# Turning 36 groups of y in a graph network's first pass and copying them back in its table pass

## The chip, the cores and the metric

One core of one Trainium2 chip. The time is device microseconds from start to end of one launch; the median of several runs is compared.

## The reference, cut to what matters

Two residual graph layers over N = 50000 nodes (128 features) and E = 25000 edges sorted by destination.

```python
h = relu(layernorm(x))
msg = concat([h[dst], h[src] - h[dst]]) @ W0 + b0
x = x + relu(segment_max(msg, dst, N))            # empty segments give 0
h = relu(layernorm(x))
a = softmax over edges of (concat([h[src] @ Wn, h[dst] @ Wn, edge @ We]) @ Watt)
g = gelu(gelu(concat([h[src], h[dst], edge]) @ Wm1 + b) @ Wm2 + b) @ Wm3 + b
x = x + scatter_add(a * g, dst)
```

The last lines leave out the projections' biases, which the kernel does add. Below, y is x after the first layer at an edge's destination, and then its normalized form.

## The kernel before, in words

The edges are cut in 49 groups of 4 tiles of 128 (G = 49, LAST = 48, GE = 512; the last group is padded). `big` holds one segment of 512 columns per group for the whole kernel (L311). Five engines each run a list of stages written out by hand, tied by semaphores. `over(engine, signal, n)` (L61) waits until the signal's stage of group n is over. `in_order` (L71) runs step m of a list: each stage at its own lag, in the order of the list. Four-slot rings (SLOTS) hold gathered rows.

**First pass.** GpSimd's `gather_a` (L518) gathers x's source and destination rows, 8 indirect DMAs a group, and waits for slot n-4 to be normalized, copied and kept. VectorE (L814) takes statistics of group n when its data are there, makes scale and shift for a pair of groups in a chain of small instructions (`norm_links`, L663; every second group), applies them (`applies`, L710: xn), scans the messages for the running maximum (`max_a`, L746) and adds x (`add_y`, L758). TensorE (L1028) runs per step: `turn_a` of the group before (8 transpositions of xn), half of the key products, `messages_a` (L1008, waits for the scan of the group before), the other half, `back_a`. ScalarE (L1184) runs: `copy_a`, `relu_a`, the signs of half the keys, `bias_a`, the other half, `norm_y_a` at lag LATE = 9, which normalizes y's rows in `big` in place, group n in step n + 9. The last 9 groups of y are normalized at the start of the table pass (`norm_y_b`, L1193).

The keys find for each edge a row of the table to which the first pass spilled y and x; SyncE's queue carries these spills and the copy of x to the output.

**Table pass.** It runs from the last group to the first (`mirrored`, L91): step n works on group 48 - n. GpSimd's `gather_b` (L537) gathers 4 tiles of the table a group and waits for xn of n-4. VectorE (L892) runs per group: xn of n-2, `spread_b(n-2)` (L869), statistics of n; after each odd n the chain for a pair. `spread_b` scans y from the bank to `hd` backwards, which spreads each destination's y to all its edges; it waits for `b_turned_y` of n, for `b_first` of n-2, whose products read that half of `hd`, and for the scan before. TensorE (L1073) runs per step n:

```python
                turn_b(n)
                turn_y_b(n + 1)
                if n >= 2:
                    turn_g_b(n - 2)
                if n >= 1:
                    first_b(n - 1)
                if n >= 2:
                    second_b(n - 2)
```

`turn_y_b` (L1031) transposes y's 4 tiles from `big` to bank 2 or 3. All transpositions have L968 in the profile, the helper `turn`. `first_b` (L1044) is 12 products of 129 columns (L1053 to L1055), `second_b` one of 512 (L1067). ScalarE (L1226) runs per step n: `relu_b(n)` (L1187), `norm_y_b(n + 2)`, `keep_g_b(n - 2)` (L1212), both halves of `gelu1_b(n - 1)`, `gelu2_b(n - 2)`, which overwrites the group's segment of `big`.

After the last group come a maximum, the exponentials, and the **output pass** (L962, L1134, L556): weighting, a scan, back turns, 196 indirect scatters by GpSimd, which wait also for the copy of x.

Of the kernel before, what the change touches and what calls it, by code (L numbers as in the profile page):

```python
# [10 lines left out]
ACT = mybir.ActivationFunctionType  # L11
AX_X = mybir.AxisListType.X

P = 128
TPG = 4
GE = TPG * P
# [44 lines left out]
def over(eng, signal, n, each=1):  # L61

    if n < 0:
        return
    if isinstance(signal, list):
        eng.wait_ge(signal[n % SLOTS], each * (n // SLOTS + 1))
    else:
        eng.wait_ge(signal, each * (n + 1))
# [11 lines left out]
def gnn_kernel(nc, x, edge_attr, W, idx_in, src_pad, dst_pad, eaT_in, wpack, out):  # L80
# [3 lines left out]
    G = TILES // TPG  # L84
# [6 lines left out]
    def mirrored(n):  # L91
        return LAST - n

    with ExitStack() as ctx:
# [3 lines left out]
        def sem(name):  # L98
            return ctx.enter_context(nc.semaphore(name))
# [51 lines left out]
        big = sb("big", [P, EP])  # L151
# [32 lines left out]
        bank = [ctx.enter_context(nc.psum_tensor(f"bank{i}", [P, 512], F32)) for i in range(8)]  # L184
# [66 lines left out]
        a_relu = sem("a_relu")  # L251
# [6 lines left out]
        a_links_y = sem("a_links_y")  # L258
        b_links_y = sem("b_links_y")
        normed_y = sem("normed_y")  # L260
        s_idx_y = sem("s_idx_y")
        s_ones_row = sem("s_ones_row")

# [1 line left out]
        b_gathered = ring("b_gathered")  # L265
        b_normed = sem("b_normed")
        b_turned_y = sem("b_turned_y")
        b_turned = sem("b_turned")
        b_hd = sem("b_hd")
        b_hs = sem("b_hs")  # L270
# [37 lines left out]
        def tile(buf, u, j):  # L308
            return buf[:, u, j * P:(j + 1) * P]

        def segment(n):  # L311
            return big[:, n * GE:(n + 1) * GE]
# [11 lines left out]
        PIECES = N // PIECE  # L324
        assert (N - PIECES * PIECE) % 16 == 0
        LATE = 9
        A_GATHERS = 2 * TPG * 16
        GATHERS = TPG * 16
        QUARTER = EP // 4
# [5 lines left out]
        def _(sp):  # L335
# [12 lines left out]
            def phases(src, eaT):  # L348
# [30 lines left out]
                def keep_xs(n):  # L379
                    over(sp, a_gathered, n, A_GATHERS)  # L380
                    sp.dma_start(table_rows(EP, n), by_tile(xs[:, n % SLOTS, :])).then_inc(a_kept[n % SLOTS], 16)
# [177 lines left out]
        def _(dve):  # L559
# [254 lines left out]
            for n in range(0, LAST):  # L814
# [5 lines left out]
                reach_a(n + 1)  # L820
                over(dve, a_gathered, n, A_GATHERS)
                stats(n, 0, tiles_a(n))
# [16 lines left out]
            add_y(LAST - 5)  # L839
            over(dve, a_gathered, LAST, A_GATHERS)  # L840
            stats(LAST, 0, tiles_a(LAST))
# [26 lines left out]

            def spread_b(n):  # L869
                d, m = n % 2, mirrored(n)  # L870
                over(dve, b_turned_y, n)
                over(dve, b_first, n - 2, 2)
                over(dve, b_hd, n - 1)
                dve.tensor_tensor_scan(hd[:, d, ::-1], flags[:, m * GE + 1:(m + 1) * GE + 1][:, ::-1],  # L874
                                       bank[2 + d][:, ::-1], hd[:, 1 - d, 0:1], ALU.mult, ALU.max
                                       ).then_inc(b_hd, 1)
# [88 lines left out]
        def _(pe):  # L965
            def turn(dest, source):
                for j in range(TPG):
                    ins = pe.transpose(dest[:, j * P:(j + 1) * P], source(j), ident[:, :])  # L968
                return ins
# [31 lines left out]
            def turn_a(n):  # L1001
                d = n % 2
                over(pe, a_normed, n)
                over(pe, a_relu, n - 2)
                turn(bank[d], lambda j: tile(xn, d, j))
                turn(bank[2 + d], lambda j: tile(xn, d, TPG + j)).then_inc(a_turned, 1)

            def messages_a(n):  # L1008
                d = n % 2
# [9 lines left out]
            def back_a(n):  # L1019
# [4 lines left out]
                else:  # L1024
# [1 line left out]
                turn(maxima(n), lambda j: tile(run, d, j)).then_inc(a_back, 1)  # L1026

            in_order(G, [(1, turn_a), (0, lambda n: keys_a(n, 0)), (2, messages_a), (0, lambda n: keys_a(n, 1)),  # L1028
                         (3, back_a)])

            def turn_y_b(n):  # L1031
                d, m = n % 2, mirrored(n)
                if n < LATE:
                    pe.wait_ge(normed_y, G - LATE + n + 1)
                over(pe, b_hd, n - 2)
                turn(bank[2 + d], lambda j: big[:, m * GE + j * P:m * GE + (j + 1) * P]).then_inc(b_turned_y, 1)

# [99 lines left out]
        def _(act):  # L1137
            act.dma_start(wp[:, :], wpack).then_inc(s_weights, 16)

            def copy_a(n):  # L1140
                over(act, a_gathered, n, A_GATHERS)
                act.activation(segment(n), xd[:, n % SLOTS, :], ACT.Copy).then_inc(a_copied, 1)

            def signs_a(n, h):
                over(act, a_keys, 2 * n + h)
                over(act, a_signs, 2 * n + h - 2)
                dest = bank[7] if h else bank[5]
                keys = dest[:, 0:2 * (KW + 1)].rearrange("p (q k) -> p q k", k=KW + 1)
                t = n * TPG + 2 * h
                for q in range(2):  # L1150
                    act.activation(compared[:, 2 * h + q, :], keys[:, q, 0:KW], ACT.Sign, bias=src_key[:, t + q:t + q + 1],  # L1151
                                   scale=-1.0, accum_out=signs[:, t + q:t + q + 1])
                act.activation(key_base[:, t:t + 2], keys[:, :, KW], ACT.Copy).then_inc(a_signs, 1)
# [13 lines left out]
            def norm_y(m):  # L1167
                for j in range(TPG):
                    c = m * TPG + j
                    rows_y = big[:, c * P:(c + 1) * P]  # L1170
                    ins = act.activation(rows_y, rows_y, ACT.Identity, scale=y_scale[:, c:c + 1],  # L1171
                                         bias=y_shift[:, c:c + 1])
                ins.then_inc(normed_y, 1)

            def norm_y_a(n):
                if n < G - LATE:
                    act.wait_ge(a_links_y, n // 2 + 1)
                    over(act, a_spilled, n, 16)
                    norm_y(n)

            act.wait_ge(s_weights, 16)
            act.wait_ge(s_keys, 1)
            act.wait_ge(s_unsorted, 1)
            in_order(G, [(0, copy_a), (1, relu_a), (0, lambda n: signs_a(n, 0)), (2, bias_a),  # L1184
                         (0, lambda n: signs_a(n, 1)), (LATE, norm_y_a)])

            def relu_b(n):  # L1187
                d = n % 2
                over(act, b_turned, n)
                over(act, b_first, n - 2, 2)  # L1190
                act.activation(hs[:, d, :], bank[d][:, :], ACT.Relu).then_inc(b_hs, 1)

            def norm_y_b(n):  # L1193
                if n < LATE:
                    m = mirrored(n)
                    if m > LAST - 7:
                        act.wait_ge(b_links_y, (n + 1) // 2 + 1)
                    else:
                        act.wait_ge(a_links_y, m // 2 + 1)
                    over(act, a_spilled, m, 16)  # L1200
                    norm_y(m)

            def gelu1_b(n, h):
                d, t = n % 2, mirrored(n) * TPG + 2 * h
# [20 lines left out]
            norm_y_b(1)  # L1225
            for n in range(0, LAST):  # L1226
                relu_b(n)
                norm_y_b(n + 2)
                if n >= 2:
                    keep_g_b(n - 2)  # L1230
                if n >= 1:
                    gelu1_b(n - 1, 0)
                    gelu1_b(n - 1, 1)
                if n >= 2:
                    gelu2_b(n - 2)
# [97 lines left out]
```

## Time and profile before

| | |
|---|---|
| median of 3 runs | 1078.14 us (1077.06 to 1079.75) |
| the profiled execution, its own time | 1078.1 us |
| its span, first to last instruction | 1076.5 us |
| mean granted TensorE clock | 0.784 |
| busy: TensorE, weight loads, VectorE, ScalarE, GpSimd | 63%, 42%, 70%, 39%, 71% |

Busy times overlap, since the engines run side by side. "DMA_INDIRECT" on POOL is the time in which GpSimd issues a gather or scatter, not the transfer. In a timeline, a row may gather several instructions (x4); the bracket is the idle time of the engine before it and what ended it. "issue" says that the profile shows nothing that was waited for.

### The profile page before, as it was taken

To read this page: it belongs to the slowest core of one execution; us is meant where nothing else is said; L and a number is where in the kernel's file an instruction comes from. 1 tells how busy PE (TensorE), PEld (TensorE's weight loads), DVE (VectorE), ACT (ScalarE), POOL (GpSimd) and SP (SyncE) were. 2 spreads that over 40 slices of the span, in tenths; PEclk is the share of its full clock that TensorE was granted. 3 is DMA by queue.
4 is the path that set the end of the run, shared out by engine and by line. 5 is a ranking of instruction groups with operands and counts; after the bars stand their busy time and mean duration, and the time that the engine had idled before them with its cause. 6 is when DMAs were issued, how large, how long until landed. Compare 5 with 4: busy or idle time off the path is not lost.

```text
span 1076.5 us, 13373 instructions
## 1 busy us (share of the span) xinstructions
PE 677.4 (63%) x3369; PEld 451.5 (42%) x3369; DVE 754.1 (70%) x2588; ACT 421.2 (39%) x1239; POOL 759.8 (71%) x796
## 2 busy tenths in 40 slices
PE   1356576565565555467549999999996555555520
PEld 1233343333333333334248888888873222222210
DVE  3468688688688788788988888888847555555540
ACT  1234445645645646646437555555552000000000
POOL 5777777777777777776277777777705777777775
PEclk9977767878887878867759999999999656555555
DMA  4645545445445555454324444443424344444420
GB/s 145 226 116 151 149 141 161 150 141 157 151 145 157 151 145 149 152 149 139 107 66 127 140 136 117 139 137 115 143 84 135 121 139 140 137 137 144 156 75 32
DMA packets 65044, 145.52 MB, mean 135 GB/s; under 512 B 17994, under 2 KB 19009, under 8 KB 64054
## 3 DMA queue, kind: packets, MB, share of 16 engines
q1 hardware_dynamic: 39734, 96.46, 27.3%
q0 software_dynamic: 25088, 47.56, 17.2%
q10 hardware_dynamic: 144, 0.63, 0.2%
q8 instruction: 28, 0.46, 0.2%
q14 instruction: 50, 0.41, 0.1%
HBM read 109.79 MB, written 64.26 MB: 162 GB/s over the span
## 4 chain that ended last, share of the span: by engine, by line
POOL 33%; DVE 30%; issue 19%; PE 8%; DMA 8%; ACT 1%; POOLq 0%; DVEq 0%; ACTq 0%
POOL out_dram L552 14%; POOL xs L484 11%; POOL xd L484 8%; DVE xn L714 8%; DVE bst L660 5%; DMA xd<-in_x_dram,idx_dst 5%; PE bank L968 4%; DVE hd L874 3%; DVE run L755 3%; DMA out_dram<-aux,idx_out 2%; DVE newton L671 2%; DVE rstd L671 2%; PE bank L1053 1%; DVE big L761 1%; PE bank L1054 1%
## 5 line engine op out<-in xcount | busy, mean ns | idle before, releaser
L552 POOL DMA_INDIRECT out_dram<-aux,idx_out x196 | 193.0, 985 | 95.2 <-issue 56.7
L484 POOL DMA_INDIRECT xs<-table,idx_y x196 | 186.4, 951 | 76.6 <-issue 55.7
L484 POOL DMA_INDIRECT xs<-in_x_dram,idx_src x196 | 187.2, 955 | 66.1 <-issue 60.6
L484 POOL DMA_INDIRECT xd<-in_x_dram,idx_dst x196 | 189.7, 968 | 59.8 <-issue 59.5
L1016 PE MATMUL bank<-hs,wp 128*128 128x512 f32 x98 | 86.0, 974 | 172.5 <-DVE run L755 172.4
L660 DVE BATCH_NORM_STATS2 bst<-xs 128x6 f32<-128x128 f32 x392 | 84.3, 278 | 105.7 <-DMA xd<-in_x_dram,idx_dst 105.1
L1100 PE MATMUL bank<-big,wp 128*128 128x512 f32 x98 | 86.3, 979 | 95.4 <-DVE bank L940 94.9
L968 PE MATMUL bank<-ident,xn 128*128 128x128 f32 x588 | 90.0, 293 | 60.8 <-DVE xn L714 59.8
L968 PEld LDWEIGHTS bank<-ident,xn 128*128 128x128 f32 x588 | 72.2, 152 | 99.1 <-DVE xn L714 86.2
L714 DVE TENSOR_SCALAR xn<-xs,mean,rstd 128x128 f32<-128x128 f32 x392 | 111.4, 366 | 1.8
L1164 ACT ACTIVATE bank<-bank,wp 128x512 f32<-128x512 f32 x49 | 32.5, 663 | 204.6 <-PE bank L1017 204.6
L956 DVE SCALAR_TENSOR_TENSOR aux<-bank,sm,xd 128x512 f32<-128x512 f32 x49 | 36.7, 748 | 106.2 <-DMA out_dram<-aux,idx_out 106.2
L1016 PEld LDWEIGHTS bank<-hs,wp 128*128 128x128 f32 x98 | 21.1, 268 | 184.8 <-issue 155.2
L968 PEld LDWEIGHTS bank<-ident,run 128*128 128x128 f32 x392 | 68.5, 192 | 66.9 <-DVE run L948 49.7
L968 PE MATMUL bank<-ident,run 128*128 128x128 f32 x392 | 87.1, 364 | 13.1 <-DVE run L948 11.7
L1151 ACT ACTIVATE compared<-bank,src_key 128x252 bf16<-128x252 f32 x196 | 90.9, 476 | 4.7 <-PE bank L997 4.6
L1171 ACT ACTIVATE big<-big,y_shift,y_scale 128x128 f32<-128x128 f32 x196 | 80.5, 492 | 9.6 <-DVE y_shift L735 9.6
L1017 PE MATMUL bank<-hd,wp 128*128 128x512 f32 x98 | 82.1, 936 | 0.0
L874 DVE TENSOR_TENSOR_SCAN hd<-flags,hd,bank 128x512 f32<-128x512 uint8 x49 | 62.5, 1276 | 27.3 <-issue 27.3
L997 PE MATMUL bank<-key_parts,m_a 100*128 100x253 bf16 x392 | 74.4, 324 | 7.8 <-DVE m_a L743 7.8
L1053 PE MATMUL bank<-wp,aux 65*128 65x129 f32 x392 | 76.6, 276 | 0.0
L1054 PE MATMUL bank<-wp,hd 128*128 128x129 f32 x392 | 76.3, 275 | 0.0
(138 smaller groups left out, 1363.3 us busy)
## 6 DMA issues: line engine op xcount, KB each, us to landing
out_dram<-in_x_dram SPq DMA_DIRECT2D x48, 512.0 KB
table<-xs SPq DMA_DIRECT2D x49, 256.0 KB, 2.2
table<-big SPq DMA_DIRECT2D x49, 256.0 KB, 4.1
xd<-table SPq DMA_DIRECT2D x49, 256.0 KB, 2.8
xn<-exps_dram SPq DMA_DIRECT2D x45, 256.0 KB, 3.3
aux<-in_src_dram SPq DMA_DIRECT2D x49, 200.0 KB
aux<-in_eaT_dram SPq DMA_DIRECT2D x49, 128.0 KB, 3.1
xs<-in_x_dram,idx_src POOLq DMA_INDIRECT x196, 3.5
```

The costliest lines, as they stand in the source:

```text
L484: pool.indirect_dma_start(tile(buf, u, j), None, source, bass.IndirectOffsetOnAxis(ap=index[:, c:c + 1], axis=0)).then_inc(done[u], 16)
L552: pool.indirect_dma_start(out, bass.IndirectOffsetOnAxis(ap=idx_out[:, c:c + 1], axis=0), tile(aux, u, j), None, bounds_check=last_row, oo ...
L660: ins = dve.bn_stats(bst[:, n % 2, first + j, :], t)
L714: ins = dve.tensor_scalar(tile(xn, k, j), t, mean[:, pair, k, j:j + 1], rstd[:, pair, k, j:j + 1], ALU.subtract, ALU.mult)
L874: dve.tensor_tensor_scan(hd[:, d, ::-1], flags[:, m * GE + 1:(m + 1) * GE + 1][:, ::-1], bank[2 + d][:, ::-1], hd[:, 1 - d, 0:1], ALU.mult ...
L968: ins = pe.transpose(dest[:, j * P:(j + 1) * P], source(j), ident[:, :])
L1016: pe.matmul(dest, weight("w0_src"), hs[:, d, :], start=True, stop=False)
L1017: pe.matmul(dest, weight("w0_dst"), hd[:, d, :], start=False, stop=True).then_inc(a_msg, 1)
L1053: pe.matmul(dest, aux[0:DE + 1, u, j * P:(j + 1) * P], weight("w1_edge"), start=True, stop=False)
L1054: pe.matmul(dest, tile(hd, d, j), weight("w1_dst"), start=False, stop=False)
L1100: pe.matmul(bank[2 + n % 2][:, :], weight("w3"), segment(n), start=True, stop=True).then_inc(c_third, 1)
L1151: act.activation(compared[:, 2 * h + q, :], keys[:, q, 0:KW], ACT.Sign, bias=src_key[:, t + q:t + q + 1], scale=-1.0, accum_out=signs[:, t ...
```

## The change

- First pass: TensorE gets a stage `turn_y_a` at lag 10, last in its step. For groups 0 to 35 (TURNED = 49 - 9 - 4 = 36) it transposes the normalized y from `big` to bank 0 or 1, after the relu that emptied that bank. ScalarE gets `keep_y_a` at lag 10, last in its step, which copies the bank back over the segment in `big`. `turn_a(n)` waits for the copy that empties its bank.
- Table pass: for groups below 36 `turn_y_b` does nothing; ScalarE's `copy_y_b(n + 1)`, after `relu_b(n)`, copies the segment to bank 2 or 3, and `spread_b` waits for that copy. The first 13 groups of this pass (48 down to 36) stay as they were.

```diff
--- before.py
+++ after.py
@@ -258,6 +258,8 @@
         a_links_y = sem("a_links_y")
         b_links_y = sem("b_links_y")
         normed_y = sem("normed_y")
+        a_turned_y = sem("a_turned_y")
+        a_kept_y = sem("a_kept_y")
         s_idx_y = sem("s_idx_y")
         s_ones_row = sem("s_ones_row")
 
@@ -265,6 +267,7 @@
         b_gathered = ring("b_gathered")
         b_normed = sem("b_normed")
         b_turned_y = sem("b_turned_y")
+        b_copied_y = sem("b_copied_y")
         b_turned = sem("b_turned")
         b_hd = sem("b_hd")
         b_hs = sem("b_hs")
@@ -324,6 +327,7 @@
         PIECES = N // PIECE
         assert (N - PIECES * PIECE) % 16 == 0
         LATE = 9
+        TURNED = G - LATE - 4
         A_GATHERS = 2 * TPG * 16
         GATHERS = TPG * 16
         QUARTER = EP // 4
@@ -868,7 +872,7 @@
 
             def spread_b(n):
                 d, m = n % 2, mirrored(n)
-                over(dve, b_turned_y, n)
+                over(dve, b_turned_y if m >= TURNED else b_copied_y, n if m >= TURNED else TURNED - 1 - m)
                 over(dve, b_first, n - 2, 2)
                 over(dve, b_hd, n - 1)
                 dve.tensor_tensor_scan(hd[:, d, ::-1], flags[:, m * GE + 1:(m + 1) * GE + 1][:, ::-1],
@@ -1002,8 +1006,16 @@
                 d = n % 2
                 over(pe, a_normed, n)
                 over(pe, a_relu, n - 2)
+                over(pe, a_kept_y, min(n - LATE - 1, TURNED - 1))
                 turn(bank[d], lambda j: tile(xn, d, j))
                 turn(bank[2 + d], lambda j: tile(xn, d, TPG + j)).then_inc(a_turned, 1)
+
+            def turn_y_a(n):
+                m = n + LATE + 1
+                if n < TURNED:
+                    pe.wait_ge(normed_y, n + 1)
+                    over(pe, a_relu, m - 2)
+                    turn(bank[m % 2], lambda j: big[:, n * GE + j * P:n * GE + (j + 1) * P]).then_inc(a_turned_y, 1)
 
             def messages_a(n):
                 d = n % 2
@@ -1026,12 +1038,14 @@
                 turn(maxima(n), lambda j: tile(run, d, j)).then_inc(a_back, 1)
 
             in_order(G, [(1, turn_a), (0, lambda n: keys_a(n, 0)), (2, messages_a), (0, lambda n: keys_a(n, 1)),
-                         (3, back_a)])
+                         (3, back_a), (LATE + 1, turn_y_a)])
 
             def turn_y_b(n):
                 d, m = n % 2, mirrored(n)
                 if n < LATE:
                     pe.wait_ge(normed_y, G - LATE + n + 1)
+                if m < TURNED:
+                    return
                 over(pe, b_hd, n - 2)
                 turn(bank[2 + d], lambda j: big[:, m * GE + j * P:m * GE + (j + 1) * P]).then_inc(b_turned_y, 1)
 
@@ -1178,11 +1192,16 @@
                     over(act, a_spilled, n, 16)
                     norm_y(n)
 
+            def keep_y_a(n):
+                if n < TURNED:
+                    over(act, a_turned_y, n)
+                    act.activation(segment(n), bank[(n + LATE + 1) % 2][:, :], ACT.Copy).then_inc(a_kept_y, 1)
+
             act.wait_ge(s_weights, 16)
             act.wait_ge(s_keys, 1)
             act.wait_ge(s_unsorted, 1)
             in_order(G, [(0, copy_a), (1, relu_a), (0, lambda n: signs_a(n, 0)), (2, bias_a),
-                         (0, lambda n: signs_a(n, 1)), (LATE, norm_y_a)])
+                         (0, lambda n: signs_a(n, 1)), (LATE, norm_y_a), (LATE + 1, keep_y_a)])
 
             def relu_b(n):
                 d = n % 2
@@ -1200,6 +1219,11 @@
                     over(act, a_spilled, m, 16)
                     norm_y(m)
 
+            def copy_y_b(n):
+                if mirrored(n) < TURNED:
+                    over(act, b_hd, n - 2)
+                    act.activation(bank[2 + n % 2][:, :], segment(mirrored(n)), ACT.Copy).then_inc(b_copied_y, 1)
+
             def gelu1_b(n, h):
                 d, t = n % 2, mirrored(n) * TPG + 2 * h
                 half = bank[4 + h][:, 0:2 * (P + 1)].rearrange("p (q c) -> p q c", c=P + 1)
@@ -1225,6 +1249,7 @@
             norm_y_b(1)
             for n in range(0, LAST):
                 relu_b(n)
+                copy_y_b(n + 1)
                 norm_y_b(n + 2)
                 if n >= 2:
                     keep_g_b(n - 2)
```

## Rows read from the trace of the kernel before

**Rows 1.** Busy time by window: length, each engine (instructions), granted clock, DMA share, GB/s.

```profile
9.30:512.07 502.77, 286.73 (x1130) 169.84 (x1130) 378.55 (x1483) 257.18 (x819) 376.92 (x392) 0.79 0.51 152
...
532.22:780.42 248.20, 223.40 (x1688) 193.38 (x1689) 209.16 (x832) 133.70 (x345) 186.41 (x196) 0.94 0.42 124
780.42:816.16 35.74, 32.35 (x215) 24.94 (x214) 18.88 (x65) 20.37 (x48) 0.00 (x0) 1.00 0.22 73
816.16:1076.50 260.34, 120.89 (x281) 54.93 (x279) 126.12 (x141) 0.00 (x0) 193.03 (x196) 0.58 0.40 124
...
642.70:652.80 10.10, 9.93 (x77) 8.58 (x77) 8.40 (x33) 5.46 (x15) 7.65 (x8) 1.00 0.45 132
```

**Rows 2.** Timeline of GpSimd in the table pass: start us, duration us, what.

```profile
597.43 0.95 POOL L484 DMA_INDIRECT xs<-table,idx_y  x1 [0.30 <-issue]
...
676.63 0.95 POOL L484 DMA_INDIRECT xs<-table,idx_y  x1 [1.42 <-issue]
...
736.90 0.95 POOL L484 DMA_INDIRECT xs<-table,idx_y  x1 [0.31 <-DVE xn L714]
...
764.45 0.95 POOL L484 DMA_INDIRECT xs<-table,idx_y  x1 [0.30 <-issue]
...
779.46 0.94 POOL L484 DMA_INDIRECT xs<-table,idx_y  x1 [0.30 <-issue]
```

**Rows 3.** Timeline of a pair of groups in the table pass, all engines.

```profile
641.49 1.11 DVE L714 TENSOR_SCALAR xn<-xs,mean,rstd 128x128 f32<-128x128 f32 x4
...
642.66 0.65 PE L968 MATMUL bank<-ident,xn 128*128 128x128 f32 x4 [0.16 <-DVE xn L714]
...
642.75 0.94 POOL L484 DMA_INDIRECT xs<-table,idx_y  x1 [0.30 <-DVE xn L714]
...
643.36 0.60 ACT L1191 ACTIVATE hs<-bank 128x512 f32<-128x512 f32 x1
...
646.97 1.28 DVE L874 TENSOR_TENSOR_SCAN hd<-flags,hd,bank 128x512 f32<-128x512 uint8 x1 [1.25 <-issue]
...
651.58 1.11 DVE L714 TENSOR_SCALAR xn<-xs,mean,rstd 128x128 f32<-128x128 f32 x4
```

**Rows 4.** One piece of the chain of waits, then timeline at the table pass's end.

```profile
540.99 2.49 DMA xs<-table,idx_y
...
769.28 0.84 DVE L660 BATCH_NORM_STATS2 bst<-xs 128x6 f32<-128x128 f32 x4
...
779.37 0.66 PE L968 MATMUL bank<-ident,xn 128*128 128x128 f32 x4 [0.52 <-DVE xn L714]
...
784.27 0.60 PE L968 MATMUL bank<-ident,xn 128*128 128x128 f32 x4
...
784.71 0.60 PE L968 MATMUL bank<-ident,big 128*128 128x128 f32 x4
...
797.96 0.60 PE L968 MATMUL bank<-ident,xn 128*128 128x128 f32 x4
```

**Rows 5.** Timeline of the first pass, all engines.

```profile
303.16 0.94 POOL L484 DMA_INDIRECT xs<-in_x_dram,idx_src  x1 [0.30 <-DVE xn L714]
...
307.30 1.28 PE L1016 MATMUL bank<-hs,wp 128*128 128x512 f32 x2 [2.80 <-DVE run L755]
...
310.32 0.66 ACT L1164 ACTIVATE bank<-bank,wp 128x512 f32<-128x512 f32 x1 [3.38 <-PE bank L1017]
...
312.13 1.64 ACT L1171 ACTIVATE big<-big,y_shift,y_scale 128x128 f32<-128x128 f32 x4
...
314.63 0.87 DVE L660 BATCH_NORM_STATS2 bst<-xs 128x6 f32<-128x128 f32 x4 [3.69 <-DMA xd<-in_x_dram,idx_dst]
...
323.34 1.09 POOL L484 DMA_INDIRECT xs<-in_x_dram,idx_src  x1 [0.30 <-DVE xn L714]
...
500.31 2.05 PE L1016 MATMUL bank<-hs,wp 128*128 128x512 f32 x2 [3.46 <-DVE run L755]
...
502.15 1.91 PE L1017 MATMUL bank<-hd,wp 128*128 128x512 f32 x2
```

## The prediction, made blind

> **What bounds the kernel now.** I read the busy time by stage first [rows 1]. The kernel is three passes one behind the other: first pass (9 to 512 us), table pass (gathers from 532 to 780, its drain to 816), output pass (816 to the end). In the output pass GpSimd issues 196 scatters in 260 us and nothing of it is touched, so time won or lost before 816 moves the end one for one.
>
> In the table pass two loops run at almost the same speed, and that is the point of the case. The first is GpSimd's: a gather starts every 1.25 us, its idle time is the fixed 0.30 between two of them, four make a group [rows 2]. From 736.90 to 779.46 it starts 34 gathers, 1.252 us each, so a pair of groups costs 10.01 at the free pace. The second is a loop through VectorE and TensorE, once per pair [rows 3]: xn of an even group is ready at 642.60; TensorE transposes xn (642.66), y and the kept gelu, and runs first_b of the group before; the scan of the next group, which writes the buffer that first_b reads, starts at 646.97, when first_b is over (the page says "issue"; by the code, L872, it is b_first); then come statistics, the rsqrt chain, and xn again at 651.58. 651.58 - 641.49 = 10.09. So TensorE has 4.3 us in a loop of 10.09, VectorE 5.8, and GpSimd, at 10.01 to 10.1, runs alongside with its ring of four full: the gather at 642.75 needs exactly the xn that ended at 642.60.
>
> In the first pass GpSimd is the wall: 16 gathers from 303.16 to 323.34, 20.18 us, 10.09 per group; VectorE waits 3.69 us per pair for data, TensorE 2.80 for a scan, ScalarE 3.38 for the message product [rows 5]. The releaser "DVE xn" beside the 0.30 is misleading there: by the code gather n waits for xn of n-4, which ended a group earlier.
>
> **The change part by part.** All against the profiled execution: span 1076.5, own time 1078.1, which is also the median of the runs shown (1078.14).
>
> 1. Table pass, removed: the 4 transpositions of y in 36 of 49 groups (n from 13, as 48 - n < 36). Four at full clock take 784.71 - 784.27 = 0.44 us [rows 4]. All lie in TensorE's 4.3 us stretch, or in the other half of the pair where they cost nothing, so the loop becomes 10.09 - 0.44 = 9.65.
>
> 2. Table pass, added: one ScalarE copy of 512 columns per group. Cost 0.60, from relu of the same size [rows 3]; bounds 0.6 and 0.7, nothing in between decides. It stands after relu (643.36 to 643.96), so it ends at 644.6 and keep_g at 645.2. The scan that needs it starts at 646.97 now, 646.53 after; the second product that needs keep_g comes after first_b. Its wait for the scan of n-2 is long over. ScalarE is 54% busy in this pass (133.7 of 248.2 us) [rows 1], so 0. If that cover were gone, at most 0.6 per pair would return.
>
> 3. So the wall of the table pass becomes GpSimd. What does the pass gain? Two terms.
> a) **GpSimd's pace.** From its gather at 597.43 (group 13) to the last at 779.46 are 143 intervals in 182.0 us [rows 2]. At the free pace, 143 x 1.252 = 179.0, so 3.0 us is the most that is to be had. Worst: the first pass's pace, 20.18 / 16 = 1.261, plus the single 1.1 us pause before 676.63, of which I find no cause: 180.3 + 1.1 = 181.4; and if gathers collide with VectorE more often than now, nothing at all or 0.5 lost. I take 0.7, with the pause kept, because the nearest stretch is that with both engines in step.
> b) **The drain.** At full ring, data wait for VectorE. The last gather of group 45 is issued at 764.45 and data land 2.49 later [rows 2, 4]: 766.94. Its statistics start at 769.28, so 2.3 us are in hand. A loop of 9.65 against a feed of 10.01 to 10.1 gains 0.4 per pair; from group 13 to 45 are 16 pairs, 6 us, more than enough to use that up. Then turn_b(45) starts at 777.0 instead of 779.37. From there TensorE is unbroken to 797.96 [rows 4] with three y transpositions in the way (46, 47, 48), 3 x 0.44 = 1.3. xn of 46, 47 and 48 move up by the same 2.3 and stay ahead. Drain: 2.3 + 1.3 = 3.6.
> Sum: 3.6 + 0.7 = 4.3 us faster.
>
> 4. First pass, added on TensorE: 36 x 4 transpositions, 0.44 at full clock, 0.88 at half, in step n+10 behind back_a. Added on ScalarE: 36 copies of 0.6. Added waits: the copy waits for that turn, and behind it on ScalarE stand copy_a and relu_a; turn_a(n) waits for the copy, and behind it on TensorE stand keys and messages. The path from one scan to the next message product, at the clock seen: 0.15 + messages 3.02 (307.30 to 310.32) + bias and signs 1.81 (to 312.13) + norm_y 1.64 + copy 0.6 + turn_a 1.1 (eight transpositions, 0.88 at full clock over 0.79) + keys 0.6 (taken as four) = 8.9, below 10.09 per group [rows 5]. What it delays (relu_a, copy_a by 0.6 to 2.8 us) has three groups of ring before GpSimd sees it. So 0; the 2.80 and 3.38 of idle shrink.
>
> 5. TensorE's clock. It is granted in full (2.4 GHz) all through the drain, where TensorE is 32.35 of 35.74 us busy, 91%, and at a mean of 0.79 in the first pass [rows 1]. Now a pair of the table pass has 9.93 us of it in 10.10 [rows 1]; after the change (9.93 - 0.88) / 10.05, about 90%, which is what the drain has. I count no loss. A loss begins when TensorE's 3.86 in the loop grows past 4.2, a mean clock under 0.92.
>
> 6. No DMA, no SyncE or GpSimd instruction moves. SyncE's eaT loads wait for first_b and come no later.
>
> **The rivals.**
> A. *GpSimd slows in its new phase.* The gather at 303.16 took 0.94, the one at 323.34 took 1.09, next to an xn [rows 5]. If data-bound step puts one such on each of 18 pairs beyond now, 18 x 0.15 = 2.7, and the pace term goes from +0.7 to -2.0: total 3.6 - 2.0 = 1.6 faster, 1076.5. The Trainium skill, SBUF — State Buffer, "Who interferes with whom", says that a tensor_scalar of VectorE in a two-port mode and GpSimd lock each other out of a shared port pair for the whole instruction. By that rule xn holds up gathers wherever they meet; the lengthened gather in the trace agrees in kind, though it lost 0.15 us and not a whole xn. Chance 0.2.
> B. *Data is not ready sooner*, since another wait of 0.4 us stands in VectorE's loop, so the catching up fails. Then only 1.3 of the drain is left, 1076.8. For it: both loops agree so closely that I may have the order of cause wrong. Against it: statistics at 769.28 show no wait. The Trainium skill, Perfetto Trace Analysis, "Identifying the Most-Contended Engine", judges TensorE by its weight loads. Taken so, it has 22% to spare in this pass (193.4 of 248.2) [rows 1] and removing its work should give nothing; I hold that a loop needs no full engine. Chance 0.15.
> C. *Slower: first pass.* The path of step 4 at half clock throughout: 0.15 + 3.7 (four passes of 0.92, from 500.31 to 502.15 are two) + 1.81 + 1.64 + 0.6 + 1.76 + 0.9 (keys, taken as four transpositions) = 10.56, over 10.09 by 0.47, 36 times: 17 us, total 17 - 4.3 = 12.8 slower, 1091. It decides once TensorE's three parts in it exceed 5.9 us, a mean clock near 0.54; 0.79 is seen, and more work is there, not less. Chance 0.09.
> D. *The change doesn't do what it says*, the scan still waiting for TensorE through the copy: the copy's input is 100 us old, so this can only be ScalarE late, at 0.6 per pair: no gain in the loop, as B. Inside B's chance.
>
> **How the numbers follow.** The likeliest case (0.56): 1078.1 - 4.3 = 1073.8, own range 1071.6 (pace term 3.0, 6.5 won) to 1074.8. A run of this kernel can tell 0.3%, 3.2 us, from no change: below 1074.9 is faster. A and B (0.35) end inside that, C slower. For 8 in 10 I reach up to A and B with some room, 1077.5, and down to 1071.2; C is left out. Faster 0.56, same 0.35, slower 0.09.
>
> **What would show it.** Right: table pass at 10.0 to 10.1 per pair still, but with VectorE's statistics waiting for gathers from about group 30 on, and the scan's "issue" wait of 1.25 down to 0.8; TensorE busy near 90% in it; last gather within 778 to 780.5; first scatter 4 us sooner, at 812; first pass unchanged to 0.5 us. Wrong: no DMA wait before statistics (B); a last gather after 780.5 (A); first pass past 512.6, or waits of VectorE for the bias (C); a granted clock under 1.00 between 600 and 780 (5).

## The result and the profile after

| | median | lowest to highest | runs |
|---|---|---|---|
| before | 1077.16 us | 1076.69 to 1079.75 | 7 |
| after | 1072.44 us | 1071.18 to 1076.93 | 7 |

The ratio is 0.9955, interval 0.9943 to 0.9966: 4.7 us faster (3.7 to 6.1). The forecast was 1073.8, faster by 4.3.

The profiled execution of after is the slowest of its seven, 1076.93 us (span 1075.3), only 1.2 under the profiled one of before. The seven runs of after go with the mean granted TensorE clock: 1071.18 at 0.800, 1072.44 at 0.787, 1076.93 at 0.773. The 29 runs of before beside e9 to e12 don't: 1076.59 at 0.784, 1080.50 at 0.799. The profiled execution of after lies far above the median, so its trace has to be read with care; a second trace of the same kernel, e7_after_again (1073.91 us, clock 0.786), stands beside it.

Busy time by window of after, where the forecast's steps can be looked up (first pass, a stretch behind it, a stretch of the table pass, table pass to the last gather, drain, output pass; the columns are those of [rows 1]):

```profile
9.30:512.07 502.77, 302.37 (x1260) 188.79 (x1261) 377.43 (x1481) 276.72 (x851) 376.82 (x392) 0.78 0.52 152
508.50:513.00 4.50, 4.26 (x12) 2.01 (x13) 2.78 (x14) 2.00 (x7) 0.00 (x0) 0.62 0.97 303
534.15:782.16 248.01, 212.44 (x1567) 182.41 (x1568) 210.96 (x837) 148.36 (x380) 184.90 (x196) 0.93 0.42 124
782.16:815.32 33.16, 29.77 (x192) 22.36 (x191) 17.54 (x60) 20.35 (x48) 0.94 (x1) 1.00 0.24 81
815.32:1075.30 259.98, 122.53 (x281) 55.71 (x279) 126.14 (x141) 0.00 (x0) 192.65 (x196) 0.57 0.41 125
655.00:660.00 5.00, 5.00 (x33) 5.00 (x31) 2.69 (x9) 2.05 (x5) 3.72 (x5) 0.66 0.23 66
```

TensorE and ScalarE have taken on the turning and keeping in the first pass (302.4 and 276.7 us against 286.7 and 257.2 [rows 1]), and the pass is as long as before. The drain has fallen from 36.70 to 33.16, measured from the last gather. Two windows, 508.5 to 513 and 655 to 660, show the clock well under 1.00; before has 1.00 in the first of them.

Next, a table of the traces on which the argument rests, in microseconds: the gap from the last gather of the first pass to the first one of the table pass, the table pass from its first gather to its last, the drain from there to the first scatter, and the rest.

| kernel | gap | table pass | drain | rest | span |
|---|---|---|---|---|---|
| before | 27.71 | 247.24 | 36.70 | 260.34 | 1076.5 |
| after | 29.84 | 248.01 | 33.16 | 259.98 | 1075.3 |
| e7, after once more | 29.59 | 245.51 | 33.56 | 259.85 | 1072.3 |
| e12, table part alone | 27.71 | 246.94 | 33.17 | 259.84 | 1072.1 |
| e9, first-pass part alone | 27.88 | 246.89 | 36.74 | 259.83 | 1075.4 |
| e10, three groups turned | 27.71 | 246.78 | 35.43 | 259.79 | 1074.7 |
| e11, twenty groups turned | 28.17 | 247.92 | 34.81 | 259.79 | 1075.0 |

**Where the gain is.** In the drain, in every trace with the whole table part: 3.1 to 3.5 us. No trace shows where the rest of the 4.7 comes from; the fastest runs of after (1071.18 to 1072.61) were not traced. **What hides it in the profiled execution.** First the gap. Timeline of after, TensorE, behind the first pass:

```profile
508.74 1.96 PE L1028 MATMUL bank<-hs,wp 128*128 128x512 f32 x2 [1.79 <-DVE run L759]
510.49 1.90 PE L1029 MATMUL bank<-hd,wp 128*128 128x512 f32 x2
```

Before has the same four matmuls at full clock:

```profile
508.95 1.10 PE L1016 MATMUL bank<-hs,wp 128*128 128x512 f32 x2 [1.61 <-DVE run L755]
509.88 1.02 PE L1017 MATMUL bank<-hd,wp 128*128 128x512 f32 x2
```

The window's clock of 0.62 is a mean: TensorE is granted either 2.4 or 1.2 GHz (1.00 or 0.50), and these rows run at 0.50 for most of it. Here nothing is hidden any more: gathers have ended, and scan, messages and bias wait for each other in turn. The next scan starts at 513.12 after 1.77 of waiting for the bias, and the first table gather comes 2.1 us later against the last one of the first pass. Second, the table pass of after. One piece of its chain of waits, the flight of the last gather of step 21:

```profile
644.04 6.06 DMA xs<-table,idx_y
```

Then timelines; VectorE and TensorE, then GpSimd:

```profile
650.13 0.87 DVE L664 BATCH_NORM_STATS2 bst<-xs 128x6 f32<-128x128 f32 x4 [1.79 <-DMA xs<-table,idx_y]
...
654.68 0.66 PE L972 MATMUL bank<-ident,xn 128*128 128x128 f32 x4 [2.44 <-DVE xn L718]
...
655.62 0.64 PE L1067 MATMUL bank<-wp,aux 65*128 65x129 f32 x2
656.05 0.64 PE L1068 MATMUL bank<-wp,hd 128*128 128x129 f32 x2
...
660.19 1.28 DVE L878 TENSOR_TENSOR_SCAN hd<-flags,hd,bank 128x512 f32<-128x512 uint8 x1 [2.46 <-issue]
...
666.67 0.94 POOL L488 DMA_INDIRECT xs<-table,idx_y  x1 [1.59 <-DVE xn L718]
...
679.31 0.94 POOL L488 DMA_INDIRECT xs<-table,idx_y  x1 [1.70 <-issue]
```

The statistics wait 1.79 for a gather. This isn't yet the wait of the forecast, for step 21 is only the ninth changed step: the gather took 6.06 us from issue to landing, where [rows 4] have 2.49. Then TensorE is idle for 2.44, its clock is at half for 3.4 us, and the products come 0.43 apart instead of the 0.22 of full clock; the scan behind them waits 2.46, so VectorE is late again and GpSimd finds its ring full (1.59 instead of 0.30). That cost 1.3 us. That the idle time brought the clock down is argued from the order alone. TensorE in e12, where the same gather took 4.88:

```profile
652.38 0.66 PE L972 MATMUL bank<-ident,xn 128*128 128x128 f32 x4 [2.26 <-DVE xn L718]
```

After an idle time of 2.26 the clock stays at 1.00 there. The 1.70 at 679.31 is a pause like the 1.42 that before has at the same place, the 114th gather of the pass [rows 2]; e7 has none. 1.3 + 1.4 is 2.7, and after's table pass is 2.5 longer than e7's.

### The profile page after: what moved, and what is told of

It reads as the page before. It is cut to its first block, busy times and chain, and to the rows that moved or that the text cites. A ratio compares the mean times of both kernels' runs of the same rounds, so it can differ in the third digit from the quotient of the medians.

```text
span 1075.3 us, 13481 instructions
## 1 busy us (share of the span) xinstructions
PE 681.5 (63%) x3369; PEld 458.6 (43%) x3369; DVE 754.1 (70%) x2588; ACT 456.5 (42%) x1311; POOL 758.9 (71%) x796
## 4 chain that ended last, share of the span: by engine, by line
POOL 37%; DVE 27%; issue 20%; DMA 8%; PE 6%; ACT 1%; POOLq 0%; DVEq 0%; ACTq 0%
POOL out_dram L556 15%; POOL xs L488 14%; POOL xd L488 8%; DVE xn L718 7%; DVE bst L664 5%; DMA xd<-in_x_dram,idx_dst 4%; DVE run L759 3%; PE bank L972 2%; DMA out_dram<-aux,idx_out 2%; DVE hd L878 2%; DVE newton L675 2%; DMA xs<-table,idx_y 2%; DVE big L765 1%; DVE rstd L675 1%; PE bank L1067 1%
## 5 line engine op out<-in xcount | busy, mean ns | idle before, releaser
L972 PE MATMUL bank<-ident,xn 128*128 128x128 f32 x588 | 98.4, 313 | 152.8 <-ACT big L1198 85.5
L972 PEld LDWEIGHTS bank<-ident,xn 128*128 128x128 f32 x588 | 76.9, 160 | 194.4 <-issue 105.7
L1028 PE MATMUL bank<-hs,wp 128*128 128x512 f32 x98 | 83.3, 946 | 75.9 <-DVE run L759 75.2
L972 PEld LDWEIGHTS bank<-ident,run 128*128 128x128 f32 x392 | 65.0, 184 | 68.2 <-DVE run L952 49.6
L972 PE MATMUL bank<-ident,run 128*128 128x128 f32 x392 | 83.6, 353 | 14.9 <-DVE run L952 11.9
L1001 PE MATMUL bank<-key_parts,m_a 100*128 100x253 bf16 x392 | 77.1, 333 | 7.7 <-DVE m_a L747 7.7
L878 DVE TENSOR_TENSOR_SCAN hd<-flags,hd,bank 128x512 f32<-128x512 uint8 x49 | 62.5, 1276 | 22.0 <-issue 22.0
L1069 PE MATMUL bank<-wp,hs 128*128 128x129 f32 x392 | 77.0, 279 | 0.0
L1029 PE MATMUL bank<-hd,wp 128*128 128x512 f32 x98 | 73.9, 848 | 0.0
```

What stands on the lines that cost most here:

```text
L1028: pe.matmul(dest, weight("w0_src"), hs[:, d, :], start=True, stop=False)
```

## The experiments

Two theories stood against each other. **L**: the table pass runs at the pace of the loop through VectorE and TensorE, GpSimd beside it at nearly the same pace; shortening the loop leaves GpSimd as the wall, and the gain is what had queued up, plus the drain. **G**: GpSimd alone sets the pace and the loop only follows. Then came **D** and **P**: is the gain in the drain and there at once (D), or does it grow with the number of changed groups (P)?

### The first four: a chip in another condition

e1_first_only copies the kept y to a spare buffer and turns in the table pass as before:

```diff
+        spare = sb("spare", [P, GE])
...
-                over(dve, b_turned_y if m >= TURNED else b_copied_y, n if m >= TURNED else TURNED - 1 - m)
+                over(dve, b_turned_y, n)
...
-                if m < TURNED:
-                    return
...
-                    act.activation(segment(n), bank[(n + LATE + 1) % 2][:, :], ACT.Copy).then_inc(a_kept_y, 1)
+                    act.activation(spare[:, :], bank[(n + LATE + 1) % 2][:, :], ACT.Copy).then_inc(a_kept_y, 1)
...
-                copy_y_b(n + 1)
```

> Only the first pass's half: TensorE turns y of 36 groups, ScalarE copies the bank to a spare buffer of its own, turn_a waits for that copy; the table pass is that of before. Theory D (the whole gain is in the drain behind the last gather; the first pass hides its half): same as before within 1 us, first pass's last gather still near 504.5. Rival C (the first pass pays for the gain): 2 us or more slower than before. Theory K (the transition between the passes is slower or faster by 1 to 2 us by the granted clock alone): the first gather of the table pass anywhere from 532 to 534.5, with the granted clock between 508 and 520 telling which.

e2_table_only leaves the turning and keeping out of the first pass, so the table pass scans y unturned:

```diff
-                over(pe, a_kept_y, min(n - LATE - 1, TURNED - 1))
...
-                         (3, back_a), (LATE + 1, turn_y_a)])
+                         (3, back_a)])
...
-                         (0, lambda n: signs_a(n, 1)), (LATE, norm_y_a), (LATE + 1, keep_y_a)])
+                         (0, lambda n: signs_a(n, 1)), (LATE, norm_y_a)])
```

> Only the table pass's half: no turn in the first pass, ScalarE copies the segments of 36 groups as they are (the turning of these y's is left out) to the bank that VectorE scans. Theory D: 4 to 5.5 us faster than before, as the whole change or up to 1 us better. Rival C: clearly better than the whole change, by 2 us or more.

e3_turned_3 and e4_turned_20 change how many groups are treated the new way, the last 3 and the last 20 steps of the table pass:

```diff
-        TURNED = G - LATE - 4
+        TURNED = 3
```

> The change for 3 groups only, the last three of the table pass (TURNED = 3). Theory D splits the gain of the drain into 1.3 us (three transpositions of y in TensorE's unbroken last stretch) and 2.3 us (a VectorE that has caught up with the gathers before the end): here only the first is left, so 1.3 us faster than before, drain from last gather to first scatter 34.4 instead of 35.7. Rival P (the gain is GpSimd's pace in the steady stretch): no more than 0.3 us. Rival E (the end alone makes it): 3.5 us or more.

> The change for 20 groups (TURNED = 20), the last 20 of the table pass, ten pairs. Theory D: a loop shorter by 0.35 to 0.44 us per pair makes up 3.5 to 4.4 us in ten pairs, which covers the 2.3 to 4 us by which data wait, so the full drain gain of 3.3 to 3.6 us: 3.5 to 4.5 us faster than before, no worse than the whole change. Rival P (pace of the gathers, in proportion to the groups): 20/36 of 4.7, 2.6 us faster.

Measured: beside these four the kernel before itself took 1319.74 us (1301 to 1343, 17 runs), 22% over all its other measurements. The four took 1377.66 (ratio 1.0495, interval 1.0413 to 1.0577), 1323.26 (1.0103, 1.0037 to 1.0169), 1323.05 (1.0081, 1.003 to 1.0131) and 1351.91 (1.0336, 1.0268 to 1.0403). Timeline of e3, TensorE and GpSimd in the first pass:

```profile
305.50 1.75 PE L972 MATMUL bank<-ident,xn 128*128 128x128 f32 x7 [11.04 <-remote]
...
306.28 0.94 POOL L488 DMA_INDIRECT xs<-in_x_dram,idx_src  x1 [3.67 <-remote]
```

The engines stand idle for reasons that the profile puts down to none of this core's work ("remote"), up to 14 us at a time on TensorE; before, after, e7, e9 and e12 have no such wait on any engine. It isn't a matter of one chip: the record gives number 13 for these four and for e5 to e8 too, beside which before took 1078.78. What caused it isn't known, nor why the first-pass part cost most there (58 us). These four runs say nothing about D or P. They were repeated as e9 to e12.

### e5 and e6: GpSimd with a quarter of its work taken away

Three gathers of four per group, in the kernel before (e5) and in the changed one (e6), one run each; the fourth tile keeps old rows:

```diff
-                gather(n, mirrored(n), xs, idx_y, table, b_gathered)
+                u = n % SLOTS
+                for j in range(TPG - 1):
+                    c = mirrored(n) * TPG + j
+                    pool.indirect_dma_start(tile(xs, u, j), None, table,
+                                            bass.IndirectOffsetOnAxis(ap=idx_y[:, c:c + 1], axis=0)
+                                            ).then_inc(b_gathered[u], 16)
...
-                    over(dve, b_gathered, n, GATHERS)
+                    over(dve, b_gathered, n, (TPG - 1) * 16)
```

> The kernel before with 3 gathers per group in the table pass instead of 4 (the fourth tile's gather is left out, so its rows are stale). GpSimd then needs 7.5 us per pair and can't be what sets the pace. Theory L (before, the loop through TensorE and VectorE sets 10.0 to 10.1 us by itself): the period stays 9.9 to 10.1 us. Rival G (GpSimd set it): 9.6 or less.

> The changed kernel with 3 gathers per group in the table pass. Theory L: the loop of TensorE and VectorE is shorter by the four transpositions, 9.60 to 9.75 us per pair in the 36 changed groups, while the first 13 groups still run at 10.0 to 10.1; the table pass ends 6 to 8 us before that of the same edit to the kernel before. Rival G: 9.0 or less, as TensorE's busy time (8.9) would allow.

Measured: e5 1079.16 us, beside 1078.78 for the kernel before; e6 1069.33. Timeline of e5 in the table pass: the first xn of three pairs, and one gather:

```profile
602.13 1.12 DVE L719 TENSOR_SCALAR xn<-xs,mean,rstd 128x128 f32<-128x128 f32 x4
...
612.21 1.11 DVE L719 TENSOR_SCALAR xn<-xs,mean,rstd 128x128 f32<-128x128 f32 x4
...
614.11 0.95 POOL L543 DMA_INDIRECT xs<-table,idx_y  x1 [2.87 <-DVE xn L719]
...
622.28 1.11 DVE L719 TENSOR_SCALAR xn<-xs,mean,rstd 128x128 f32<-128x128 f32 x4
```

GpSimd needs 6 x 1.25 = 7.5 us for a pair now and waits for its ring, 2.87 in the row shown and up to 3.4; the pair still takes 10.07. Theory G falls: a quarter less work for the engine that is 75% busy gave nothing. The same view of e6:

```profile
601.23 1.11 DVE L723 TENSOR_SCALAR xn<-xs,mean,rstd 128x128 f32<-128x128 f32 x4
...
611.30 1.11 DVE L723 TENSOR_SCALAR xn<-xs,mean,rstd 128x128 f32<-128x128 f32 x4
...
620.89 1.11 DVE L723 TENSOR_SCALAR xn<-xs,mean,rstd 128x128 f32<-128x128 f32 x4
...
630.48 1.11 DVE L723 TENSOR_SCALAR xn<-xs,mean,rstd 128x128 f32<-128x128 f32 x4
```

The first pair is still of the old kind, with TensorE's y transpositions: 10.07. From the step where they end it is 9.59. Four transpositions shortened the loop by 0.48 (forecast 0.44). The table pass fell from 244.11 to 236.04: with the feed out of the way the change is worth 9.8 us, twice as much.

### e7: the changed kernel once more

> The changed kernel once more, for a second trace. Theory K (TensorE's granted clock is what differs between the 1076.9 us of the profiled run and the 1071 to 1072.6 of the others): a run near 1071.5 shows the clock in full between 508 and 513, no stretch below full between 640 and 780, the first gather of the table pass near 532.2 and the last at or before 780. Rival: the same clock and the same two late stretches in a run near 1071.5, the difference being somewhere else.

Measured: 1073.91 us, one run. Timeline of e7, VectorE, in the table pass, then GpSimd's last gather and first scatter:

```profile
697.12 0.87 DVE L664 BATCH_NORM_STATS2 bst<-xs 128x6 f32<-128x128 f32 x4 [1.04 <-DMA xs<-table,idx_y]
...
717.23 0.87 DVE L664 BATCH_NORM_STATS2 bst<-xs 128x6 f32<-128x128 f32 x4 [0.82 <-DMA xs<-table,idx_y]
...
739.91 1.11 DVE L718 TENSOR_SCALAR xn<-xs,mean,rstd 128x128 f32<-128x128 f32 x4
...
744.95 1.28 DVE L878 TENSOR_TENSOR_SCAN hd<-flags,hd,bank 128x512 f32<-128x512 uint8 x1 [0.82 <-issue]
...
749.97 1.12 DVE L718 TENSOR_SCALAR xn<-xs,mean,rstd 128x128 f32<-128x128 f32 x4
...
778.89 0.94 POOL L488 DMA_INDIRECT xs<-table,idx_y  x1 [0.30 <-issue]
812.45 1.02 POOL L556 DMA_INDIRECT out_dram<-aux,idx_out  x1 [32.62 <-DVE aux L960]
```

The statistics of steps 31 and 35 wait for data, 1.04 and 0.82, and no others do: the last gathers of these two took 3.58 and 3.63 us to land. From 739.91 to 749.97 a pair takes 10.06; the seven pairs from 700.51 on take 9.57 to 10.67, 9.95 in the mean. The scan's wait is 0.82 where it was 1.25 [rows 3]. VectorE has no arrears left: the last gather of step 41 lands at 746.23 and its statistics start at 746.26. This is the state that the forecast describes. The gap is 29.59, with the clock at 0.63 from 508.5 to 513, as in the profiled execution; the table pass has no fall of the clock and no pause near 677. Theory K's condition, a run near 1071.5, wasn't met. The two late stretches of the table pass account for most of the 3.0 us between the two traces; e7 with before's gap would be near 1072.0, an estimate from the table.

### e8: without the copy to the bank

VectorE scans y from its segment in SBUF, ScalarE's copy of the table pass is left out:

```diff
-                    over(dve, b_turned_y if m >= TURNED else b_copied_y, n if m >= TURNED else TURNED - 1 - m)
+                    if m >= TURNED:
+                        over(dve, b_turned_y, n)
+                    else:
+                        over(dve, a_kept_y, m)
...
-                                       bank[2 + d][:, ::-1], hd[:, 1 - d, 0:1], ALU.mult, ALU.max
+                                       (bank[2 + d] if m >= TURNED else segment(m))[:, ::-1], hd[:, 1 - d, 0:1], ALU.mult, ALU.max
...
-                copy_y_b(n + 1)
```

> The changed kernel without ScalarE's copy in the table pass: VectorE scans the segment in SBUF itself. Theory L: the copy was hidden, so nothing to win by leaving it out, within 0.7 us of the whole change. Rival S (a VectorE scan with both inputs in SBUF is slower, or holds up GpSimd's gathers): the scan over 1.3 us or gathers over 1.27 us apart, and 2 us or more slower than the whole change. Rival A (the copy does cost, relu and keep_g late): 1 us or more faster than the whole change.

Measured: 1091.31 us (1088.39 to 1092.19), ratio 1.0107 (1.0094 to 1.0121), some 17 to 19 us over the whole change. The table pass takes 264.38. Groups by line of e8 between 600 and 780 (two groups), and a piece of its timeline:

```profile
L488 POOL DMA_INDIRECT xs<-table,idx_y x130 | 140.7, 1082 | 39.6 <-issue 32.6 <-DVE xn L718 7.0
...
L881 DVE TENSOR_TENSOR_SCAN hd<-flags,hd,big 128x512 f32<-128x512 uint8 x30 | 38.4, 1281 | 8.8 <-issue 8.7
```

```profile
697.52 1.28 DVE L881 TENSOR_TENSOR_SCAN hd<-flags,hd,big 128x512 f32<-128x512 uint8 x1
...
697.75 1.81 POOL L488 DMA_INDIRECT xs<-table,idx_y  x1 [0.30 <-DVE xn L718]
699.86 0.94 POOL L488 DMA_INDIRECT xs<-table,idx_y  x1 [0.30 <-issue]
```

The same group of gathers in e7, between 600 and 780:

```profile
L488 POOL DMA_INDIRECT xs<-table,idx_y x144 | 136.7, 949 | 43.9 <-issue 40.2 <-DVE xn L718 3.7
```

The scan is as long as ever (1281 ns, from the bank 1276), but a gather that meets it takes 1.81 instead of 0.94, and the mean of all rises from 949 to 1082 ns. 130 gathers fit where e7 has 144. The trace holds its own comparison: in the first 13 groups, where the scan still reads a bank, no gather takes over 1.03; of the 144 behind them 25 take over 1.2, each of them while a scan of a segment runs. Their mean is 0.13 above e7's, and 144 x 0.13 is the 19 us by which this table pass is longer (264.38 against 245.51); TensorE's clock falls in this pass too (0.50 from 677 to 678), but nothing is left over for that to explain. So the copy, free on an engine with room, is what keeps the scan off GpSimd. The Trainium skill (SBUF — State Buffer, "Who interferes with whom") says that a VectorE instruction with two SBUF inputs contends with a GpSimd instruction that reads SBUF; flags and segment are two such inputs, and this run agrees.

### e9 to e12: the first four again

> The first pass's half alone (as in e1), on a chip where the kernel before takes its usual time. Theory D: the first pass hides its half, same as before within 1 us. Rival C: 2 us or more slower. Last gather of the first pass within 0.7 us of 504.5; a first gather of the table pass between 532 and 534.5.

Measured: 1077.15 us (1076.43 to 1079.07, 11 runs) beside 1077.31, ratio 0.9998 (0.9989 to 1.0007). The first pass hides the turning and the keeping, to within about a microsecond.

> The change for the last 3 groups of the table pass only (as in e3). Theory D: the three transpositions in TensorE's unbroken last stretch alone, 1.3 us faster than before, drain from the start of the last gather to the first scatter 35.4 instead of 36.7. Rival P (the gain is the pace of the gathers): no more than 0.3 us. Rival E (the end alone makes it): 3.5 us or more.

Measured: 1076.23 us, ratio 0.9993 (0.9984 to 1.0003). The median can't be told from no change; the trace can: the drain is 35.43, 1.27 less than before. Three groups bring the part of the drain that needs only three.

> The change for the last 20 groups of the table pass only (as in e4). The loop of 10.07 becomes 9.60 in ten pairs, 4.7 us of catching up against 4 us or less by which data wait. Theory D: 3.5 to 4.7 us faster than before, drain 33.1 to 33.6, equal to the whole change within 1 us. Rival P, in proportion to the groups: 2.6 us faster, 2 us short of the whole change.

Measured: 1075.43 us (12 runs), ratio 0.9979 (0.9969 to 0.9988): 1.3 to 3.3 faster. That is nearer to P (the gain grows with the groups) than to D. In its trace (1076.67 us, above its median) the drain is 34.81 instead of 33.2. Two pieces of the chain of waits of e11 show two late gathers, the last ones of steps 19 and 45:

```profile
632.61 6.58 DMA xs<-table,idx_y
...
765.42 3.92 DMA xs<-table,idx_y
```

And the timeline of e11, a pause of GpSimd and VectorE's statistics of group 45:

```profile
677.72 0.94 POOL L488 DMA_INDIRECT xs<-table,idx_y  x1 [2.05 <-issue]
...
769.37 0.87 DVE L664 BATCH_NORM_STATS2 bst<-xs 128x6 f32<-128x128 f32 x4 [1.35 <-DMA xs<-table,idx_y]
```

The last gather of group 45 landed after 3.92 us, where [rows 4] have 2.49, and the statistics had to wait for it: VectorE had caught up, and 1.4 of the 1.65 that the drain lacks is this flight. The gather of step 19 made the still unchanged loop wait 1.10, its pair took 11.31 and the next ones 10.06 and 10.05, and GpSimd lost 0.6 at 644.57; with the longer pause (2.05 for 1.43) that is about the 1.1 by which the table pass is longer than in e9 and e10. But late transfers in one trace don't make a median. A cause that would is that a loop without slack in its first 29 steps can't make up what late gathers and such pauses cost it; that was not tried.

> The table pass's half alone (as in e2; y of 36 groups is left unturned, so the products get it row-wise). Theory D: 4 to 5.5 us faster than before, equal to the whole change within 1 us. Rival C: better than the whole change by 2 us or more.

Measured: 1073.35 us (1072.98 to 1075.7, 6 runs), ratio 0.9965 (0.9952 to 0.9979). The table part alone gives the gain of the whole change within 1 us, and what its trace shows of it is in the drain (33.17 against 36.74 in e9).

### The drain taken apart

Timelines of TensorE: the transpositions of xn for group 45, at the end of the table pass. First after, then e10:

```profile
779.84 0.66 PE L972 MATMUL bank<-ident,xn 128*128 128x128 f32 x4 [0.94 <-DVE xn L718]
```

```profile
779.42 0.66 PE L972 MATMUL bank<-ident,xn 128*128 128x128 f32 x4 [0.49 <-DVE xn L718]
```

Together with the last gather of group 45 and the first scatter of each trace they give two stretches:

| kernel | last gather of group 45 | to TensorE's turn of it | from there to the first scatter |
|---|---|---|---|
| before | 764.45 | 14.92 | 36.79 |
| e9, first-pass part | 763.86 | 14.92 | 36.79 |
| e10, three groups | 764.50 | 14.92 | 35.49 |
| e12, table part | 764.04 | 12.74 | 35.48 |
| after | 767.09 | 12.75 | 35.48 |
| e7, after once more | 763.82 | 13.14 | 35.49 |
| e11, twenty groups | 765.42 | 14.31 | 35.48 |

The second column is VectorE's arrears: 2.2 won where it has caught up (1.8 in e7), nothing with three groups. The third is TensorE's unbroken stretch: 1.30 won by the three transpositions that stood in it, in each trace to a hundredth.

## Why the prediction was right, and where not

- **Direction and size**: right, 4.7 (3.7 to 6.1) for 4.3, inside the range and inside the likeliest case's own. That the two are so near is in part luck: the traces show the 3.6 of the drain, but neither the 0.7 of the pace nor where the rest of the 4.7 lies. The forecast also counts from 1078.1; the median of seven runs of before is 1077.16, 0.9 lower.
- **Step 1**, loop 10.09 to 9.65: right. e5 and e6 show it bare: 10.07 to 9.59.
- **Step 2**, the copy hidden: right as a cost. The scan's wait fell by the loop's gain (1.25 to 0.82). What the step didn't ask is why the copy is there; without it 17 to 19 us are lost (e8).
- **Step 3a**, GpSimd's pace, 0.7 with bounds of -0.5 and 3.0: not borne out, and miscounted. From 597.43 to 779.46 are 144 intervals, not 143 (597.43 is the last gather of step 12). At the free pace they take 180.3, so 1.7 was the most to be had, 1.1 of it the pause; the likeliest case's low end then is 1072.8 and not 1071.6, just above what was measured. Against before single traces give +0.3 (e12), +1.7 (e7, which lacks the pause) and -0.8 (after). But e9 and e10, whose table passes are unchanged but for the last three groups of e10, have 246.89 and 246.78, and e12 on the same chip has 246.94: nothing gained. e7's lack of the pause needn't be the change's doing, since e5, which has before's loop, lacks it too. The term can't be told from nought.
- **Step 3b**, the drain, 3.6: measured 3.5 in after and in e12, 3.1 in e7. Its terms: 2.3 catching up, measured 2.2 (1.8 in e7); 1.3 for three transpositions, measured 1.3. The statement that catching up is "more than enough" with 16 pairs is not the whole of it: in e11 the steps from 29 to 45 are 8 pairs, 8 x 0.4 = 3.2 us, on paper also more than 2.3, and yet it brought about 2 in all. By the forecast's own working it should have brought 3.6. In its trace VectorE did catch up; what was lost there was lost to gathers that landed late, for which the forecast took 2.49 throughout. Whether that holds for the median stays open.
- **Step 4**, first pass for nothing: right (e9). Rival C falls.
- **Step 5**, the clock: wrong as worked out. It took the mean activity of a pair, 90%, and compared it with the drain. In fact TensorE is 92% busy in e7 with its clock full, but a loop that waits for a late gather gets single gaps of over 2 us. After the one of 2.44 in the profiled execution the clock was at half for 3.4 us; after 2.07 in e8 it fell too, after 2.26 in e12 it didn't. The mark set for "wrong", a granted clock under 1.00 between 600 and 780, did show, in one of the two traces of the kernel, and cost 1.3 us. The stretch at 508.5 to 513 wasn't foreseen at all: the gap is 2 us longer in the two traces in which the clock is low there.
- **Rival A**, GpSimd slows: falls for this change; its gathers take 949 ns in e7 and 948 in before (135.58 us for 143 between 600 and 780). It appears in earnest when both inputs of the scan lie in SBUF.
- **Rival B**, data not ready sooner: falls by the waits at 697.12 and 717.23 and by the second column above. Its reading of TensorE's weight loads as room to spare (the Trainium skill, Perfetto Trace Analysis, "Identifying the Most-Contended Engine") fails here: 0.44 us taken off an engine with 78% of weight loads took 0.48 off every pair (e6).
- **What would show it**: last gather and first scatter at 778.89 and 812.45 in e7, forecast 778 to 780.5 and 812; first wait of the statistics at step 31, forecast about 30, though only two of them wait, and late gathers made them wait from step 21 in after and e12. In the profiled execution last gather and first scatter came at 782.16 and 815.32, the scatter 3.3 later than forecast: 2.1 are the gap, 1.3 what followed the late gather of step 21.

## What to carry to other kernels

Where two loops of nearly equal speed run side by side, as here, shortening one is worth what its engine was in arrears when the feed ends, plus what stood in the unbroken drain, and little more; work that part out row by row, since the mean of busy time shows none of it. Taking a quarter of the work from the busier engine (e5) is the quick proof of which loop leads. And before a seemingly useless copy into a PSUM bank is removed, look at which engine is held up when its reader takes both inputs from SBUF: here the copy was worth 17 to 19 us. Count intervals between rows twice before a bound rests on them; one gather too few made 3.0 out of 1.7 here.

## What the runs showed of the hardware

- A scan with both inputs in SBUF stretched the gathers that GpSimd issued meanwhile from 0.94 to 1.81 us, without getting longer itself; with one input in a PSUM bank it left them alone.
- After an idle time of 2.44 us in after TensorE's granted clock was at half, 1.2 instead of 2.4 GHz, for 3.4 us (rows 655.62 to 658.63 are at the slower pace), though it was over 90% busy on average. The length of the idle time alone doesn't decide: 2.07 in e8 was followed by a fall, 2.26 in e12 and 2.16 in e11 were not.
- The last gather of a group, 128 rows, landed 2.49 (before), 2.59 (after) and 2.60 us (e7) after its issue where it was quick, but after 6.06 (after), 4.88 and 5.33 (e12) and 6.58 (e11) in single rows of the table pass; no cause was found.
- Behind the first pass the clock from 508.5 to 513 was 1.00 in before and in e5, e6, e8, e9, e10, e11 and e12, and 0.62 and 0.63 in after and e7. Since e6 and e8 have the very first pass of after, the change doesn't bring it about each time; whether it makes it more frequent stays open. The gap was 2 us longer with it.
- A pause of GpSimd of 1.1 to 1.75 us over the usual 0.30 stands before the 114th gather of the table pass in before, after and e9 to e12 (these four on chip 11), and not in e5 to e8 (on chip 13); no cause was found.
- Beside e1 to e4 the kernel before took 1320 us, with idle time put down to "remote" in the traces of the four, and 1079 beside e5 to e8 on a chip of the same number. A comparison there would have called each part of the change slower. That the kernel before runs beside each experiment is what showed it.
